# Seven half-size products instead of eight for a decoder layer's context keys and values

## What is computed

```python
k_ctx = (h_ctx_kv @ wk_ctx).reshape(B, T, NUM_KV_HEADS, HEAD_DIM)
v_ctx = (h_ctx_kv @ wv_ctx).reshape(B, T, NUM_KV_HEADS, HEAD_DIM)
k_ctx = rms_norm(k_ctx, k_norm_w)
```

## Time and profile before

| | |
|---|---|
| three timed runs | 2698.4, 2698.48, 2699.3 us |
| span of the profiled execution (first to last instruction) | 2697.1 us |
| PE busy in that span | 98% |
| stage `phase_context`, PE from its first matmul | 12.4 to 551 us |
| DVE, ACT busy in that stage | 36%, 41% |
| mean DMA rate in that stage | 141 GB/s |

### The profile page before, as it was taken

One profiled execution on the slowest core, in us unless ns is written; L12 is line 12 of the kernel. 1 busy time (PEld: TensorE's weight loads), 2 busy tenths in 40 slices (PEclk: granted clock), 3 DMA queues, 4 the chain that ended last, 5 costly groups with the idle time before them and its releaser, 6 DMA issues.

```text
span 2697.1 us, 39689 instructions
## 1 busy us (share of the span) xinstructions
PE 2654.4 (98%) x15112; PEld 2472.0 (92%) x15112; DVE 1702.9 (63%) x2377; ACT 1160.4 (43%) x2035; POOL 0.9 (0%) x9
## 2 busy tenths in 40 slices
PE   8999999999999999999999999999999999999997
PEld 7989889989999999998889999989998998999997
DVE  4333333368777776568788888746973772763766
ACT  4333333444444444335456666623541341431432
POOL 0000000000000000000000000000000000000000
PEclk9999999999999999999999999999999999999999
DMA  6444444521111112107135555513122121121122
GB/s 211 133 132 132 132 132 132 173 75 48 64 64 64 50 61 76 63 32 160 47 126 167 169 171 169 148 51 109 63 66 76 63 70 56 63 79 63 63 94 96
DMA packets 117226, 266.02 MB, mean 99 GB/s; under 512 B 19822, under 2 KB 86254, under 8 KB 102894
## 3 DMA queue, kind: packets, MB, share of 16 engines
q1 hardware_dynamic: 117102, 264.31, 31.0%
HBM read 206.63 MB, written 57.66 MB: 98 GB/s over the span
## 4 chain that ended last, share of the span: by engine, by line
PE 87%; DVE 9%; issue 2%; ACT 1%; DMA 0%; DVEq 0%; SPq 0%; ACTq 0%
PE PS L2815 6%; PE PS L2813 6%; PE PS L2817 6%; PE PS L2310 5%; PE PS L131 4%; PE PS L129 4%; PE PS L130 4%; PE PS L469 3%; PE PS L470 3%; PE PS L471 3%; PE PS L444 3%; PE PS L445 3%; PE PS L446 3%; PE PS L2323 3%; PE PS L2850 3%; PE PS L2849 3%
## 5 line engine op out<-in xcount | busy, mean ns | idle before, releaser
L2941 ACT ACTIVATE WH<-RAW 128x512 fp32r<-128x512 f32 x180 | 113.4, 631 | 222.2 <-PE PS L2817 119.8
L131 PE MATMUL PS<-XH,WL 128*128 128x512 f32 (+1 forms) x592 | 204.4, 345 | 0.0
L129 PE MATMUL PS<-XH,WH 128*128 128x512 f32 (+1 forms) x592 | 204.1, 345 | 0.0
L444 PE MATMUL PS<-CH,KWH 128*128 128x338 f32 (+1 forms) x512 | 167.9, 328 | 12.4 <-DVE CL L420 12.4
L3174 DVE TENSOR_TENSOR WL<-RAW,WH 128x512 fp32r<-128x512 f32 x196 | 134.6, 687 | 58.5 <-ACT WH L2941 55.2
L130 PE MATMUL PS<-XL,WH 128*128 128x512 f32 (+1 forms) x496 | 170.1, 343 | 0.0
L445 PE MATMUL PS<-CL,KWH 128*128 128x338 f32 (+1 forms) x512 | 167.8, 328 | 0.0
L446 PE MATMUL PS<-CH,KWL 128*128 128x338 f32 (+1 forms) x512 | 167.7, 328 | 0.0
L2815 PE MATMUL PS<-XL,WH 128*128 128x400 f32 x480 | 166.0, 346 | 0.0
L2813 PE MATMUL PS<-XH,WH 128*128 128x400 f32 x480 | 164.8, 343 | 0.8 <-issue 0.6
L2817 PE MATMUL PS<-XH,WL 128*128 128x400 f32 x480 | 165.0, 344 | 0.0
(11 more groups left out here) (423 smaller groups left out, 7561.0 us busy)
## 6 DMA issues: line engine op xcount, KB each, us to landing
RAW<-weights_dram SPq DMA_DIRECT2D x111, 1024.0 KB, 4.9
values_scratch<-VS SPq DMA_DIRECT2D x40, 512.0 KB, 7.5
a_KHL<-keys_scratch SPq DMA_DIRECT2D x32, 411.0 KB, 5.0
keys_scratch<-KS SPq DMA_DIRECT2D x16, 768.0 KB, 6.3
R<-context_dram SPq DMA_DIRECT2D x8, 1352.0 KB, 6.9
keys_scratch<-KS SPq DMA_DIRECT2D x16, 676.0 KB, 5.7
R<-context_dram SPq DMA_DIRECT2D x7, 1536.0 KB, 7.0
XH<-values_scratch SPq DMA_DIRECT2D x16, 640.0 KB
```

The source lines that it names most:

```text
L129: pe.matmul(out, wh, xh[:, k, cols], start=(k == 0), stop=False)
L131: mm = pe.matmul(out, wl, xh[:, k, cols], start=False, stop=(k == KT - 1))
L444: pe.matmul(out, wh, CH[e][:, k, 0:w], start=(k == 0), stop=False)
```

## The change

Batches are no longer kept apart: the 5776 tokens are cut into 12 groups, eleven of 512 and, at index 10, one of 144. Within a group, tokens are halved (h), features are halved (j), and the output heads are halved (i: even and odd key heads, first and last two value heads). Keys and values of a group are then each a 2 by 2 product of blocks, computed by seven block products (Winograd's form of Strassen's scheme) where the plain form has eight.

- **Weights.** The seven left factors A11, A21+A22-A11, A21+A22, A11-A21, A12, A22 and A12-(A21+A22-A11) are made once, split, and stay in `WALL` in high and low parts, for keys and for values. DVE makes the sums for the keys (`mix`), GpSimd (POOL) those for the values.
- **Tokens.** Of the four quarters of a group's tokens DVE makes T1 to T4 in place (`moving_sum`, L668), four operations of 1024 elements. Each of the seven moving operands is split (`moving_hi`; `moving_lo`, L647), 1024 elements. They lie in two slots of `WH`, `WL` and one of `XC`; each slot is used again when the values of the product before in it are done.
- **Products.** `keys(g, p)` is 2 heads by 4 k-tiles by 3 matmuls of 256 columns (72 in the small group); `values(g, p)` is 2 token tiles (one in the small group) by 4 by 3 matmuls of 256 columns. Key products go to banks 0 to 2, value products to banks 3 to 5; two products are accumulated onto an earlier one.
- **Outputs.** ACT keeps product 0 (`keep_key`, `keep_value`). DVE then forms u2, u3 and the output blocks c22, c21, c12 for keys (`key_combine`, L697) and values (`value_combine`, L728), 512 elements each; block 11 is read from its bank. Key heads are normed as before, in four steps of 512 columns, a group later. The variance matmuls of heads 0 and 1 stand behind the keys of product 0, those of heads 2 and 3 behind the keys of product 2.
- **Stores.** `store_keys` and `store_values` cut at batch borders, and `store_values` also at the multiples of 128 tokens of each batch, since `values_scratch` is laid out by batch. A combination that overwrites `KS` or `VS` waits for the former group's stores (`k_stored`, `v_stored`). In the last tile of a batch 14 further rows are filled from tile rows 0 to 13.
- **Behind the stage.** The last group's variances stand in the first retention unit, and the loads of x and of the retention's first weights move.

The diff, cut (`...` marks what is left out):

```diff
@@ -37,8 +37,12 @@
 PARTS = ((0, 512), (512, NT))
 CTX = 722
 KEYS = CTX + T
-CA = 384
-CB = CTX - CA
+NTOK = B * CTX
+GROUPS = 12
+SMALL = GROUPS - 2
+FULL = 512
+SMALL_N = NTOK - FULL * (GROUPS - 1)
+WIDE = FULL // 2
...
+        WALL = sb("WALL", [P, PRODUCTS, 2, 2 * UNIT], F32R)
...
+        start = [FULL * g if g <= SMALL else NTOK - FULL * (GROUPS - g) for g in range(GROUPS)]
+        width = [SMALL_N // 2 if g == SMALL else WIDE for g in range(GROUPS)]
+        tiles = [-(-w // P) for w in width]
+        BANK, OPENS = (0, 1, 2, 1, 0, 1, 2), (True, True, True, True, False, True, False)
...
+        def pieces(n0, n):
+            out, at = [], n0
+            while at < n0 + n:
+                end = min(n0 + n, (at // CTX + 1) * CTX)
+                out.append((at // CTX, at % CTX, at - n0, end - at))
+                at = end
+            return out
...
+        def tile_pieces(n0, n):
+            out = []
+            for b, at, row, count in pieces(n0, n):
+                while count > 0:
+                    take = min(count, P - at % P)
+                    out.append((b, at // P, at % P, row, take))
+                    at, row, count = at + take, row + take, count - take
+                if at == CTX:
+                    out.append((b, SELF_C, SELF_P, 0, SELF_STORED - SELF_P))
+            return out
...
+            a11, a21, a12, a22 = (value_weight_source(p) for p in (0, 2, 4, 5))
+            s3 = value_weight_source(3)
+            pool.wait_ge(first_v, 16)
+            pool.tensor_tensor(s3, a11, a21, ALU.subtract).then_inc(wv_mix, 1)
+            pool.wait_ge(c.raw[1], 16)
...
+            pool.tensor_tensor(a21, a21, a22, ALU.add).then_inc(wv_mix, 1)
...
+            pool.wait_ge(wv_lo, 1)
+            pool.tensor_tensor(a11, a21, a11, ALU.subtract).then_inc(wv_mix, 1)
...
+            def load(g):
+                if g > 1:
+                    sp.wait_ge(cx_seq, seq_at(g - 2, "lo6"))
+                sp.dma_start(source(g), c.context[:, :, start[g]:start[g] + 2 * width[g]]
+                             ).then_inc(x_raw[g % 2], 16)
...
+            def store_keys(g, n):
+                sp.wait_ge(k_out, 8 * g + (4 * n + 4))
+                for b, at, col, count in pieces(start[g], 2 * width[g]):
+                    for part in range(2):
+                        dst = c.kscr[b, 1 - n::2, :, part, at:at + count]
+                        sp.dma_start(dst.rearrange("v p t -> p v t"),
+                                     ki[:, 1 - n, :, part, col:col + count].bitcast(F32)
+                                     ).then_inc(k_stored[n], 16)
...
+            def store_values(g, h):
+                sp.wait_ge(outs, out_at(g, "lo12" if h else "lo21"))
+                for t, each in enumerate(half_tiles(g, h)):
+                    for b, k, at, row, count in each:
+                        dst = c.vscr[b, :, at:at + count, k]
+                        sp.dma_start(dst.rearrange("v p s d -> p v (s d)"),
+                                     VS[row:row + count, h, t].bitcast(F32)
+                                     .rearrange("p v s d -> p v (s d)")).then_inc(v_stored[h], 16)
...
+            sp.dma_start(key_weight_source(0), half(0, 0)).then_inc(first_w, 16)
+            sp.dma_start(quarter(0, 0, 0), c.context[:, 0:QUAD, 0:WIDE]).then_inc(first_in[0], 16)
+            sp.dma_start(value_raw[:, 1, :], c.weights[2]).then_inc(first_v, 16)
+            sp.dma_start(key_weight_source(2), half(0, 1)).then_inc(c.raw[0], 16)
+            sp.dma_start(key_weight_source(5), half(1, 0)).then_inc(c.raw[0], 16)
+            sp.dma_start(source(0)[:, :, WIDE:FULL],
+                         c.context[:, :, WIDE:FULL]).then_inc(first_in[1], 16)
+            sp.dma_start(value_raw[:, 0, :], c.weights[3]).then_inc(c.raw[1], 16)
+            sp.dma_start(quarter(0, 1, 0), c.context[:, QUAD:KT, 0:WIDE]).then_inc(x_raw[0], 16)
+            sp.wait_ge(c.raw[1], 16)
+            sp.dma_start(key_weight_source(4), half(1, 1)).then_inc(c.raw[1], 16)
+            load(1)
...
+            for g in range(GROUPS):
+                if g > 0:
+                    store_values(g - 1, 1)
...
+                    store_keys(g - 1, 0)
+                    store_keys(g - 1, 1)
+                if g < GROUPS - 2:
+                    load(g + 2)
+                elif g == GROUPS - 2:
+                    sp.wait_ge(cx_seq, seq_at(g, "lo6"))
+                    sp.dma_start(c.R[:, 0:QUAD, :], c.x[:, 0:QUAD, :]).then_inc(c.x_in[0], 16)
+                else:
+                    sp.wait_ge(cx_seq, seq_at(g, "lo6"))
+                    for s in range(2):
+                        sp.dma_start(c.RAW[:, s, :], c.weights[U_RET // 2 + s]).then_inc(c.raw[s], 16)
+                store_values(g, 0)
+            store_values(GROUPS - 1, 1)
+            sp.wait_ge(c.w_lo, U_RET + 2)
             sp.dma_start(c.RAW[:, 0, :], c.weights[U_RET // 2 + 2]).then_inc(c.raw[0], 16)
-            sp.wait_ge(chunk_lo, 2 * B + 1)
...
+                elif which == "c22":
+                    dve.wait_ge(outs, out_at(g, "u3K"))
+                    dve.wait_ge(k_done, done_at(g, 2))
+                    if g > 0:
+                        dve.wait_ge(k_stored[0], k_stored_by(g))
+                    out, x, y = keys_at(g, 1, 1, LOW).bitcast(F32), key_sum(g, 3), key_bank(g, 2)
...
+                hi, lo = moving(g, p)
+                for j in range(2):
+                    out = key_bank(g, BANK[p])[:, j, :]
+                    for k in range(QUAD):
+                        wh, wl = (key_weight(p, part)[:, j, k * P:(k + 1) * P] for part in range(2))
+                        pe.matmul(out, wh, hi[:, k, :], start=(OPENS[p] and j + k == 0), stop=False,
+                                  skip_group_check=True)
+                        pe.matmul(out, wh, lo[:, k, :], start=False, stop=False,
+                                  skip_group_check=True)
+                        mm = pe.matmul(out, wl, hi[:, k, :], start=False, stop=(k == QUAD - 1),
+                                       skip_group_check=True)
...
+                for t in range(tiles[g]):
+                    rows = min(P, width[g] - P * t)
+                    cols = slice(P * t, P * t + rows)
+                    out = c.PS[0:rows, 3 + BANK[p], WIDE * t:WIDE * (t + 1)]
+                    for k in range(QUAD):
+                        wh, wl = (value_weight(p, part)[:, 2 * P * k:2 * P * (k + 1)]
+                                  for part in range(2))
+                        pe.matmul(out, hi[:, k, cols], wh, start=(OPENS[p] and t + k == 0),
+                                  stop=False, skip_group_check=True)
+                        pe.matmul(out, lo[:, k, cols], wh, start=False, stop=False,
+                                  skip_group_check=True)
+                        mm = pe.matmul(out, hi[:, k, cols], wl, start=False, stop=(k == QUAD - 1),
...
+            for g in range(GROUPS):
+                for p in range(PRODUCTS):
+                    pe.wait_ge(cx_seq, seq_at(g, f"lo{p}"))
+                    keys(g, p)
+                    if p == 0 and g > 0:
+                        variance(g - 1, 0)
+                        variance(g - 1, 1)
+                    if p == 2 and g > 0:
+                        variance(g - 1, 2)
+                        variance(g - 1, 3)
+                    values(g, p)
 
...
-                act.wait_ge(before.k_stored, 16 + 64 * B)
-                act.wait_ge(before.v_stored, 16 + 96 * B)
+                for n in range(2):
+                    act.wait_ge(before.k_stored[n], before.K_STORED[n])
+                    act.wait_ge(before.v_stored[n], before.V_STORED[n])
...
                 pe.wait_ge(c.made, 4)
-                pe.wait_ge(before.k_out, 4 + 8 * B - 2)
-                unit_matmuls(c, pe, 0, 0, XH, XL, lambda h, k: pe.wait_ge(c.x_lo, k + 1),
-                             k_first=True)
+                pe.wait_ge(before.kept, 3 * GROUPS)
+                pe.wait_ge(before.outs, before.out_at("c21K"))
+
+                def ready(h, k):
+                    pe.wait_ge(c.x_lo, k + 1)
+                    if h == 0 and k == 2:
+                        before.last_variance(pe, 0)
+
+                unit_matmuls(c, pe, 0, 0, XH, XL, ready, k_first=True)
+                before.last_variance(pe, 1)
...
-    put(*(_unit(a["L0_xattn_wk_ctx"], v * HD) for v in range(KV_N)))
-    put(_values(a["L0_xattn_wv_ctx"], 0, KV_N * HD))
+    kw, vw = a["L0_xattn_wk_ctx"].reshape(2, KT // 2, P, 2, 2, HD), a["L0_xattn_wv_ctx"].reshape(
+        2, KT // 2, P, 2, 2 * HD)
+    for i, j in ((0, 0), (1, 0), (1, 1), (0, 1)):
+        put(kw[j, :, :, :, i].transpose(1, 2, 0, 3).reshape(P, UNIT))
+    for i, j in ((0, 0), (1, 0), (0, 1), (1, 1)):
+        put(vw[j, :, :, i].transpose(1, 0, 2).reshape(P, UNIT))
```

(20 more changed lines are left out.)

880 lines of the change are left out of this document (586 added, 294 removed).

## The result

The changed kernel takes **2712.2 us** (2710.9 to 2712.9 in four runs) beside 2698.6 us of the kernel before (2698.4 to 2699.3): ratio 1.0049, 95% interval 1.0035 to 1.0064. It is slower by 13.6 us.

The account below looks back on a forecast made before the run. PE (TensorE), busy 98% of the span, was taken as the bound. From 2698.5 us, -48.7 + 4 + 8 + 37 + 24 = +24 gave 2723 us; its own range was 2695 to 2765, with rival 1 2656 to 2765.

Parts of the forecast that it names:

- PE's work: Edited stage: matmul time falls from 535.9 to 487.2 us, with 256-column matmuls 0.120 apart and 72-column ones 0.075: -48.7 us.
- small waits of DVE's and ACT's order: Squares of heads 2 and 3 meet the variance matmuls with about 1 us to spare: +4 us over twelve groups.
- the start: PE starts at 8.4 instead of 12.4 us, then idles before product 1 for its value weights and restarts slowly: +8 us.
- key c22 and value u3, three times: Groups 2, 3 and 5: PE waits 5.8, 9.5 and 10.5 us behind late key stores, plus three restarts of 3.8: +37.
- the stage's end: First retention head: ACT waits for the last group's stores, landed at 53 us, and PE's transposes wait for ACT: +24 us.
- Rival 3: A 128-column weight load is the floor under a matmul's distance, at 0.132 us: 45 us more, 2768 us; chance 0.05.
- The value stores: Stores of 82, 46 or 118 partitions go to the same two DMA engines, 44.5 ns per 1 KB packet, and don't keep up.
- Rival 1: Odd value stores spread over all engines, or other ones each time, and both waits vanish: 2662 us; chance 0.18.
- turning point: Waits vanish once the key store lands by 32 us of a group, with two half groups' stores under 30 us together.
- Rival 2: Two engines alone run faster, or second-half stores are taken early, so only the last wait stays: 2685 to 2700; chance 0.07.

Follow-up runs that it names:

- split16: The changed kernel with every value store cut into a multiple of 16 rows and a rest under 16 (82 = 80 + 2): 2655.6 us.
- split_last: The changed kernel with the last group's value stores alone cut into a multiple of 16 rows and a rest: 2693.9 us.
- four_engines: The changed kernel with value stores of 82, 46 and 118 rows cut 76 + 6, 44 + 2 and 116 + 2: 2655.1 us.
- one_engine: The changed kernel with value stores of 82, 46 and 118 rows cut into two of 41, 23 and 59: 2877.1 us.

## Why the prediction was right, point by point

Forecast 2723, measured 2712.2: slower, for the reasons given, but by about half of the forecast's 24 us. The terms against the profile:

| term | forecast | measured |
|---|---|---|
| PE's work | -48.7 | about -55.1 |
| small waits of DVE's and ACT's order | +4 | +0.3 |
| the start | +8 | +10.5 |
| key c22 and value u3, three times | +37 | +34.5 |
| the stage's end | +24 | +21.8 |
| sum | +24.3 | +12.0 |

**PE's work.** Measured as what is left of the stage's -9.8 us; counted from the distances (3780 x 0.1168, 168 x 0.111 and 21 for the variances, against 535.9) it is -54.8. Two sizes were off, in opposite directions. The 256-column distance is 0.1168, not 0.120: 3780 x 0.0032 = 12 us less (the forecast's 42.1 us a group was 41.05). It had the better row in hand, three matmuls in 0.35 us, and set it aside since their weight loads were smaller. The 72-column distance was taken as 0.075 and is 0.111: 168 x 0.036 = 6 us more. That step failed because 100 columns at 0.087 were taken as an upper bound for 72. The weights there have 100 columns and not 128. The kernel before has the other case too, 100 columns moved over weights of 128, at 1097 us, with four distances in 0.45 us:

```profile
1097.45 0.28 PE L1785 MATMUL PS<-QK,VHL 100*128 100x100 f32 x1
...
1097.90 0.28 PE L1786 MATMUL PS<-QK,VHL 100*128 100x100 f32 x1
```

That is about 0.111 again, as with 72 and 128 columns: among these matmuls it is the weights' columns that count. Rival 3 was right that there is a floor and wrong on where it lies. It was also wrong that loads are busy 0.188 us whatever the matmul: those of 128 columns are about that, those of the score matmuls with 100 columns take 0.17. The Trainium skill, "TensorE: Matmul & The Clock Gate", section "LDWEIGHTS (loading the stationary operand)", puts a weight load at its columns / 1.2 ns, by which 128 columns are an estimated 107 ns and 100 columns 83. The measured 0.111 and 0.087 us both lie 4 ns above that and agree with it.

**The start.** PE starts at 8.97 (forecast 8.4), waits 12.6 us before product 1 (9.1) and pays some 1.6 and 1.9 us of slow matmuls, 25.1 in all. The chain was the forecast one: A22 is there at 17.3 (16.0), two POOL additions, then high and low parts. What the sum missed is that POOL and DVE hold each other up, shown above. It also misread the kernel before, whose start it put at 12.4 + 3.8 = 16.2, with 26 slow matmuls. The trace has 14:

```profile
12.85 0.52 PE L445 MATMUL PS<-CL,KWH 128*128 128x384 f32 x1
...
16.37 0.52 PE L444 MATMUL PS<-CH,KWH 128*128 128x384 f32 x1
16.69 0.45 PE L445 MATMUL PS<-CL,KWH 128*128 128x384 f32 x1
16.98 0.33 PE L446 MATMUL PS<-CH,KWL 128*128 128x384 f32 x1
17.15 0.34 PE L444 MATMUL PS<-CH,KWH 128*128 128x384 f32 x1
```

From 12.39 to 16.98 there are 14 distances; at 0.173 they would take 2.4 us, so that start costs 2.2 us, not 3.8, and ends at 14.6. The change makes the start 10.5 us longer. That 8 came near it is in part luck: the same 3.8 was also put on product 1's restart, which takes 1.9.

**The value stores.** Right in the mechanism: two engines, the same two each time, 42.3 ns a packet for 44.5; waits of 6.0, 11.3 and 11.4 us in groups 2, 3 and 5 for 5.8, 9.5 and 10.5; none in groups 6 to 10. Each restart is 1.8 to 2.1 us instead of 3.8. The 3.8 came from the miscount at the start of the kernel before: 14 distances of 384 columns, each 0.147 us longer, cost there 2.2 us, and 17 to 20 of 256 columns, each 0.096 longer, cost nearly the same here.

**The end.** The first transposes start 57.2 us behind the stage's end; the forecast said 56.8. But they would now be due at 40.1 (measured in split16 and split_last), not at 37.0:

```profile
544.79 1.95 PE L143 MATMUL PS<-ID,W 128*100 128x128 f32 x16
```

This row of split16 stands 40.1 us behind its first retention matmul at 504.7. The last group's variances now lie in those units, and 1.0 us of a wait for DVE (L99). So the wait is 17.0 instead of 19.8, and 3.1 us of the end's cost are not the stores'. With them gone, split16 keeps that part.

**Small waits.** 0.3 us instead of 4: the squares of heads 2 and 3 do meet the variances with little to spare, 0.3 us late once.

**Rival 1** (stores spread, 2662) is what split16 made true: 2655.6. The forecast's sum without the store terms was 6 us too high: by PE's work (6.4) and the small waits (3.7), less what the start (2.5) and the shifted variances (3.1) took more. That leaves 1.7 us unexplained. Its turning point, stores of two half groups under 30 us, agrees with four_engines (15 to 21 us, no wait) and with group 6 of the changed kernel, which has the 25 us of group 5's stores before it and doesn't wait. **Rival 2** (only the last wait stays) didn't happen.

The saving of columns was thus real, about 55 us. The stores took back nearly as much: 28.6 and 17.0 us of waits, 5.9 and 1.7 of restarts, 53.2 in all (the spans of the changed kernel and of split16 are 55.3 apart; the other 2 us weren't traced). The start took 10.5 and the shifted variances 3.1, and that is the loss. The forecast erred by 12 us in all: four of its five terms were too high, by 6.4, 3.7, 2.5 and 2.2, and only the start too low, by 2.5.

## What to carry to other kernels

When tiles are moved off their old boundaries, look at the outer sizes of every DMA that the change cuts anew: here 82 and 46 rows instead of 128 made a copy of the same bytes take eight times as long, and an uneven cut into 80 + 2 and 32 + 14 mended it at once. Ask of such a transfer not its bytes but what the most loaded engine carries, and compare that with the time until the next user: below the threshold it costs nothing (25 us of stores in a group here), above it each microsecond is paid (32.5 us more of stores gave 32.4 more of waiting in one_engine), and it may be paid by a transfer of another kind whose share on that engine comes behind. And halving the columns of a matmul pays only down to the weight load: from 256 to 128 columns the distance falls only from 0.117 to 0.111 us. One more level of the same trick within groups of 512 tokens needs 7 x 6 matmuls of 128 columns for 24 of 256, so by these distances PE's time there would rise by an estimated two thirds.

## What the runs showed of the hardware

- Stores of 82, 46 or 118 rows run on two engines at 24 GB/s each (48 GB/s from 112 to 134 us), stores of 41, 23 or 59 rows on one (24 GB/s in one_engine), the same ones each time, and other transfers of the queue run beside them on the other engines. The Trainium skill, "DMA: Bandwidth & Descriptors", section "Why a DMA increments its semaphore by 16 and not by 1", states that the engines of such a copy are the largest number up to 16 that divides its slowest dimension, and the lowest-numbered ones; 48 and 24 GB/s agree with it.
- POOL's additions and DVE's operations on two SBUF tiles exclude each other here. POOL's of 1024 elements take 2.35 and 3.20 us and DVE's beside them 2.28 and 3.35, where DVE's alone take 1.22. The starts and ends fit a strict alternation: POOL's first ends at 19.73, DVE's at 20.82, 1.1 later; POOL's second at 23.02, DVE's at 24.09, again 1.1 later. The other two additions show the same distance (11.55 and 12.63, 45.58 and 46.66). The Trainium skill, "SBUF — State Buffer", section "SBUF: two separate sides", calls the port pair that the two share an exclusive lock, held for a whole instruction, and these rows agree.
- Behind each of the waits of 6.0, 11.3, 11.4 and 12.6 us PE's 256-column matmuls first stand 0.213 apart and then 0.117. Behind the last of these the granted clock is 0.51, the level of 1.2 GHz, until 33.0 us and 1.00, that of 2.4, from there on:

```profile
28.90:33.00 4.10, 4.10 (x19) 4.10 (x20) 3.50 (x3) 1.97 (x4) 0.00 (x0) 0.51 0.00 0
33.00:37.00 4.00, 4.00 (x36) 4.00 (x35) 3.32 (x3) 2.84 (x4) 0.00 (x0) 1.00 0.02 4
```

The restart costs 1.6 to 2.2 us in each of the seven places read: after waits of 2.4, 6, 11 and 12.6 us and at the programs' starts, with 256 or 384 columns.
- The distance of matmuls with 128 x 128 weights is 0.228, 0.173, 0.155, 0.117, 0.111 and 0.111 us for 512, 384, 338, 256, 128 and 72 columns. For 100 columns it is 0.111 with weights of 128 columns and 0.087 with weights of 100. These are products; transposes weren't compared.
